# The one-hots of the repeated pairs are built on ScalarE, and most of a histogram is summed there: a graph network on one Trainium2 core

## The reference, cut to what matters

```python
x = layernorm(x + L0(x, src, dst, ...))          # one attention layer, softmax over the edges of a node
x = layernorm(x + L1(x, [src, dst], edge_attr_128, ...))   # edge_aggr = zeros.at[src].add(edge_attr_128), then an MLP
x = layernorm(x + L2(x, [src, dst], edge_attr_3, ...))     # three attention layers
x = layernorm(x + L3(x, src, dst, ...))
# L3, five times: agg = segment_sum(h[src], dst); h = relu(bn(relu(bn((h + agg) @ W1 + b1)) @ W2 + b2)) ...
```

## Time and profile before

| what | value |
|---|---|
| time, median of 3 runs | 9828.47 us (9817.87 to 9830.84) |
| the profiled execution | 9827.57 us |
| its span, first to last instruction | 9826.3 us |
| busy in it: PE / DVE / ACT / POOL | 6388.6 / 4378.2 / 3263.5 / 4526.1 us |
| `positions()` | about 175 to 484.8 us |
| `sort_rows()` | 484.8 to 1596.5 us |

### The profile page before, as it was taken

The page is one execution under the profiler, slowest core; times in us unless marked ns, Lnnn a source line. Parts: engine busy times, 40 slices in busy tenths (PEclk is TensorE's granted clock), DMA queues, the critical chain, the costliest instruction groups (busy, mean ns, idle before and its releaser), DMA issues. The chain is left out here.

```text
span 9826.3 us, 148779 instructions
## 1 busy us (share of the span) xinstructions
PE 6388.6 (65%) x38246; PEld 4633.5 (47%) x38247; DVE 4378.2 (45%) x11659; ACT 3263.5 (33%) x5847; POOL 4526.1 (46%) x4475
## 2 busy tenths in 40 slices
PE   1720003747768865766657665766659898989896
PEld 1710003722258844666656665666634444444443
DVE  3880003579977775555545554555540202020203
ACT  1000000049967744444444444444420202020202
POOL 2887777567720005777577774777710000000001
PEclk8555556878889987888888997888879898989898
DMA  4423336747754412333233332333336464646463
GB/s 112 110 83 106 105 104 165 205 135 209 209 170 122 128 49 66 85 84 84 67 88 85 84 84 70 84 84 84 85 92 202 124 202 127 200 127 199 128 199 112
DMA packets 1108444, 1192.58 MB, mean 121 GB/s; under 512 B 118455, under 2 KB 993350, under 8 KB 1107768
## 3 DMA queue, kind: packets, MB, share of 16 engines
q1 hardware_dynamic: 711988, 630.75, 21.9%
q0 software_dynamic: 150784, 336.22, 14.6%
q10 hardware_dynamic: 245444, 222.71, 8.1%
HBM read 974.87 MB, written 216.86 MB: 121 GB/s over the span
## 5 line engine op out<-in xcount | busy, mean ns | idle before, releaser
L1190 POOL DMA_INDIRECT ring<-gat_rows,src_idx x2496 | 2415.1, 968 | 1002.4 <-issue 999.7
L1311 PE MATMUL ps<-ring,xT_b 128*128 x8192 | 1289.5, 306 | 975.0 <-ACT xT_b L1397 971.0
L1311 PEld LDWEIGHTS ps<-ring,xT_b 128*128 128x128 f32 x8192 | 1115.2, 211 | 1107.1 <-issue 1103.7
L1389 ACT ACTIVATE xT_a<-xT_a,state 128x514 f32<-128x514 f32 x1024 | 740.0, 723 | 1865.9 <-SPq L1162 1270.1
L1301 PE MATMUL ps<-ident,s_col 128*128 128x128 f32 x8192 | 1228.5, 299 | 190.1 <-DVE s_col L1326 116.8
L1301 PEld LDWEIGHTS ps<-ident,s_col 128*128 128x128 f32 x8192 | 1142.8, 215 | 211.9 <-DVE s_col L1326 115.9
L1820 POOL TENSOR_TENSOR features<-xT_a,features 128x640 bf16<-128x640 f32 x50 | 82.6, 1656 | 2431.6 <-ACT features L1817 2431.2
L1617 PE MATMUL ps<-xT_b,features 128*128 128x504 f16 (+1 forms) x5655 | 1198.3, 367 | 0.0
L1359 DVE CUSTOM_DVE_ANT_0 xT_a<-ps,mask,xT_a 128x512 f32<-128x512 f32 x1024 | 765.8, 748 | 713.4 <-PE ps L1301 494.5
L684 POOL DMA_INDIRECT by_src<-ring,state x832 | 848.6, 1020 | 254.8 <-issue 253.1
L1461 PE MATMUL ps<-ring,xT_b 128*128 x2048 | 276.9, 304 | 982.1 <-DVE xT_b L1470 885.2
(11 more groups left out here) (376 smaller groups left out, 8012.3 us busy)
## 6 DMA issues: line engine op xcount, KB each, us to landing
dl_all<-dloc_rows ACTq DMA_DIRECT2D x1052, 128.0 KB, 3.1
xT_b<-adjacency SPq DMA_DIRECT2D x145, 882.0 KB, 4.7
xT_b<-adjacency SPq DMA_DIRECT2D x145, 756.0 KB, 4.6
adj_tile<-adjacency SPq DMA_DIRECT2D x102, 882.0 KB
adjacency<-xT_b ACTq DMA_DIRECT2D x319, 252.0 KB
adj_tile<-adjacency SPq DMA_DIRECT2D x100, 756.0 KB
ring<-by_src SPq DMA_DIRECT2D x52, 1040.0 KB
ring<-gathered SPq DMA_DIRECT2D x208, 260.0 KB
```

Source lines behind the costliest of these rows:

```text
L1190: pool.indirect_dma_start(ring[:, o:o + RC], None, table[:, :], bass.IndirectOffsetOnAxis(src_idx[:, t * W + u:t * W + u + 1], 0)).then_in ...
L1311: m = pe.matmul(bank(BO + v % 2, R), pw[v % 4][:, w * P:(w + 1) * P], ring[:, w * RC:][:, bass.ds(look(SLOT, u - 7), R)], start=w == 0, st ...
L1389: act.activation(um[u % 4], sm[u % 8], ACT.Identity, bias=S[:, ER:][:, bass.ds(look(BC, u), 1)]).then_inc(q["act_a"], 1)
```

## The change

In the first pass of `positions()`, of every three chunks DVE still compares and sums the first. For the other two it only compares, and ACT sums the hits by a Copy with an accumulator output. `extra_counts()` keeps DVE's preparation but for three conversions and a subtraction that go and two scalings that come (`at` becomes -`at`, `block` becomes 1 - `block`), drops the comparisons of line 630, and returns a function `make(v)` that builds tile v on ACT: Abs of (index + `at`) over 128 columns, Abs of (index + `block`) over 50, then Relu of (1 - x) over both, 178 columns of bf16, into one of eight buffers. `sort_rows()` calls it from group `LATE` = 12 on, 9 or 10 tiles behind each group's two copies, so that the 832 tiles are spread over 92 groups. PE multiplies tile by tile, and DVE's 52 copies out of PSUM stay.

```diff
--- before.py
+++ after.py
@@ -78,6 +78,7 @@
 assert QT * P == QC and NQ * QC == EH
 DUMP = NB * P
 RG = 4
+LATE = 12
 NT = 5
 WD = 504
 NWIN = -(-(NB * P) // WD)
@@ -540,11 +541,24 @@
                 load(n)
             for c in range(NQ):
                 dve.wait_ge(q[f"ld{c % 2}"], 32 * (c // 2 + 1))
-                if c >= 2:
-                    dve.wait_ge(q["eq"], c - 1)
-                dve.tensor_scalar(hit[c % 2], blk[c % 2], binid, 0.0, ALU.is_equal, ALU.add,
-                                  accum_out=hist[:, c:c + 1]).then_inc(q["eq"], 1)
+                if c % 3 == 0:
+                    if c >= 2:
+                        dve.wait_ge(q["eq"], c - 1)
+                    if c >= 3:
+                        dve.wait_ge(q["act_a"], c // 3 * 2 - 1)
+                    dve.tensor_scalar(hit[c % 2], blk[c % 2], binid, 0.0, ALU.is_equal, ALU.add,
+                                      accum_out=hist[:, c:c + 1]).then_inc(q["eq"], 1)
+                else:
+                    if c >= 2:
+                        dve.wait_ge(q["eq"], c - 1)
+                    if c >= 3:
+                        dve.wait_ge(q["act_a"], (c - 2) // 3 * 2 + (c - 2) % 3)
+                    dve.tensor_scalar(hit[c % 2], blk[c % 2], binid, None, ALU.is_equal).then_inc(q["eq"], 1)
+                    act.wait_ge(q["eq"], c + 1)
+                    act.activation(hit[c % 2], hit[c % 2], ACT.Copy, accum_out=hist[:, c:c + 1]
+                                   ).then_inc(q["act_a"], 1)
             dve.wait_ge(q["eq"], NQ)
+            dve.wait_ge(q["act_a"], NQ - -(-NQ // 3))
             s(dve, lambda: dve.tensor_reduce(total, hist, AX.X, ALU.add))
             s(pe, lambda: pe.matmul(PS[:, 1024:1025], before, total, start=True, stop=True))
             s(dve, lambda: dve.tensor_copy(first, PS[:, 1024:1025]))
@@ -602,14 +616,11 @@
 
             at, block = XTa[:, 3072:3072 + ET], XTa[:, 3072 + ET:3072 + 2 * ET]
             whole = XTa[:, 3072 + 2 * ET:3072 + 3 * ET].bitcast(I32)
...
+            room = 3072 + 2 * ET
+            size = P + NBP
+            one = [XTa[:, room + i * size // 2:room + (i + 1) * size // 2].bitcast(BF16) for i in range(8)]
+            off = [XTa[:, room + 4 * size + i * size:room + 4 * size + (i + 1) * size] for i in range(2)]
+            whole = XTa[:, 3072 + 2 * ET:3072 + 3 * ET].bitcast(I32)
...
-            s(dve, lambda: dve.tensor_copy(whole, at))
-            s(dve, lambda: dve.tensor_copy(at_b, whole))
-            s(dve, lambda: dve.tensor_scalar(block_b, block, 1.0, None, ALU.subtract))
-            s(dve, lambda: dve.tensor_copy(iota_b, iota_row[:, :]))
-            s.wait(dve)
-
-            def equal(out, n, ids):
-                return dve.tensor_tensor(out, iota_b[:, 0:n].rearrange("p (a n) -> p a n", a=1).to_broadcast([P, 8, n]),
-                                         ids.rearrange("p (t a) -> p t a", a=1).to_broadcast([P, 8, n]), ALU.is_equal)
-
-            def evict(r):
-                dve.wait_ge(q["product"], 2 * r + 2)
+            s(dve, lambda: dve.tensor_scalar(block, block, -1.0, 1.0, ALU.mult, ALU.add))
+            s(dve, lambda: dve.tensor_scalar(at, at, -1.0, None, ALU.mult))
+
+            def make(v):
+                if v == 0:
+                    s.wait(act)
+                if v >= 8:
+                    act.wait_ge(q["product"], v - 7)
+                act.activation(off[v % 2][:, 0:P], iota_row[:, :], ACT.Abs, bias=at[:, v:v + 1])
+                act.activation(off[v % 2][:, P:size], iota_row[:, 0:NBP], ACT.Abs, bias=block[:, v:v + 1]
+                               ).then_inc(q["act_a"], 1)
+                act.wait_ge(q["act_a"], v + 1)
+                act.activation(one[v % 8], off[v % 2], ACT.Relu, bias=1.0, scale=-1.0).then_inc(q["eq"], 1)
+
+            for r in range(NV):
+                dve.wait_ge(q["product"], (r + 1) * RUN)
                 dve.tensor_copy(extra[:, r * NBP:(r + 1) * NBP], PS[:, r % 4 * 512:r % 4 * 512 + NBP]
                                 ).then_inc(q["evac"], 1)
-
-            for g in range(2 * NV):
-                if g >= 3:
-                    dve.wait_ge(q["product"], g - 2)
-                equal(node[g % 3], P, at_b[:, g * 8:(g + 1) * 8])
-                equal(home[g % 3], NBP, block_b[:, g * 8:(g + 1) * 8]).then_inc(q["eq"], 1)
-                if g >= 4 and g % 2 == 0:
-                    evict(g // 2 - 2)
-            for r in (NV - 2, NV - 1):
-                evict(r)
-            s.wait(pe)
-            for g in range(2 * NV):
-                r = g // 2
-                if g % 2 == 0 and r >= 4:
+            for v in range(ET):
+                r = v // RUN
+                if v % RUN == 0 and r >= 4:
                     pe.wait_ge(q["evac"], r - 3)
-                pe.wait_ge(q["eq"], g + 1)
-                for u in range(8):
-                    m = pe.matmul(PS[:, r % 4 * 512:r % 4 * 512 + NBP], node[g % 3][:, u, :], home[g % 3][:, u, :],
-                                  start=g % 2 == 0 and u == 0, stop=g % 2 == 1 and u == 7)
-                m.then_inc(q["product"], 1)
+                pe.wait_ge(q["eq"], v + 1)
+                pe.matmul(PS[:, r % 4 * 512:r % 4 * 512 + NBP], one[v % 8][:, 0:P], one[v % 8][:, P:size],
+                          start=v % RUN == 0, stop=v % RUN == RUN - 1).then_inc(q["product"], 1)
+            return make
 
         def sort_rows():
 
@@ -669,7 +672,7 @@
                 if g == RG:
                     edge_scores(s)
                     source_steps(s)
-                    extra_counts(s)
+                    make = extra_counts(s)
                 src = rows_of[g * L1U * P:(g + 1) * L1U * P, :] if g < n - 1 else tail_rows
                 for eng in (sp, act):
                     if g >= RG:
@@ -677,6 +680,9 @@
                 sp.dma_start(buf(b)[:, :, 0:D], tiled(src)).then_inc(q[f"ld{b}"], 16)
                 for o, t in ((D, src_cols), (D + 1, dst_cols)):
                     act.activation(buf(b)[:, :, o], t[:, g * L1U:(g + 1) * L1U], ACT.Copy).then_inc(q["stage"], 1)
+                if g >= LATE:
+                    for v in range((g - LATE) * ET // (n - LATE), (g - LATE + 1) * ET // (n - LATE)):
+                        make(v)
                 pool.wait_ge(q[f"ld{b}"], 16 * (g // RG + 1))
                 pool.wait_ge(q["stage"], 2 * (g + 1))
                 settled(pool)
```

## The result

The changed kernel takes 9791.37 us (median of 5 runs, 9779.2 to 9792.79) against 9828.47 of the kernel before (5 runs, 9817.87 to 9830.85): ratio 0.9959, 95% interval 0.9946 to 0.9973. It is faster by 37 us, 0.4%; forecast were 9784 us. Lines behind the changed functions now have a number higher by 6; the scatter of line 684 is line 690.

The account below looks back on a forecast made before the run. POOL's successive instructions bound the scatter; DVE and PE end the numbering, POOL close behind. From 9827.57 us, -43.5 and -1.3 give 9782.8, or 9784 against the median, 0.45% less; range 9773 to 9801.

Parts of the forecast that it names:

- Line 630 and POOL: Scatter in `sort_rows()`: without line 630 on DVE, 116 scatters take 959 instead of 1334 ns, saving 43.5 us.
- The 10.3 us that the copies out of PSUM might have cost: Scatter: line 635's 52 copies of 199 ns, if each held POOL for its whole length; nothing was taken for them.
- ACT's tile: Scatter: two Abs and a Relu take ACT 925 ns a tile, 8.8 us in POOL's 10.1 a group, costing nothing.
- ACT the bound: Rival in the scatter: tiles above 1.117 us make ACT late; at 1.19 us, 60 us more, 9844 us. Chance 0.08.
- The table loads: Rival on ACT: Abs and Relu evict each other's tables, two loads of 1.283 us a tile, 11900 us. Chance 0.02.
- The numbering: `positions()`: -3.85 us from the earlier end plus 2.5 for comparisons, so -1.3 us (-3.85 to +8.9).
- The release behind POOL's last store: End of the numbering: POOL's last store, issued by 478.63, plus 2.33 us landing and barrier, gives 480.96 instead of 484.81.
- the size that had been taken for the comparisons: Numbering: 17 new DVE comparisons hold POOL by chance for 3.8 us together; 2.5 us were taken.
- The first pass: First pass of `positions()`: 2.97 us a chunk instead of 3.54, near 88 us instead of 103.
- the 14.7 us: Numbering: DVE's gain over 26 chunks, of which at most 3.85 count; rival that it shows in full, 9771 us, chance 0.03.
- a full lock: Rival in the numbering: POOL's gathers wait out each of 17 new comparisons, 12.7 us, giving 9794 us. Chance 0.08.
- What one of them saves or costs is carried to the end: Whole kernel: stages are parted by barriers, so the touched stages' differences, -43.5 and -1.3 us, reach the end.

Follow-up runs that it names:

- LATE = 40: The changed kernel with lower bounds on registers, ACT's tiles starting at group 40 instead of 12 (13 a group): 9942.73 us, one run.
- bounds only: The kernel before with a lower bound of 1 on registers that semaphore waits compare with: 9836.7 us, ratio 1.0004 to the kernel before.
- no counts, bounds: The changed kernel with register bounds, repeated-pair counts left out (no tiles, products or copies; `extra` set to 0): 9805.53 us, ratio 0.9959 to the kernel before.
- histogram only, bounds: The kernel before with register bounds and only the histogram's change, one-hots staying on DVE: 9836.67 us, ratio 1.0001.
- counts only, bounds: The kernel before with register bounds and only the one-hots' change, the histogram staying wholly on DVE: 9810.85 us, ratio 0.9979.
- change, bounds, pause: The changed kernel with register bounds and twelve 640-column index fills on POOL behind the last scatter: 9857.52 us, ratio 1.0015 to the kernel before.
- change, bounds: The changed kernel with a lower bound of 1 on registers that semaphore waits compare with: 9848.5 us, ratio 1.0015 to the kernel before.
- change, bounds, FIRST = 24: The changed kernel with register bounds, 24 instead of 32 tiles gathered in the numbering, the rest in the source sums: 9851.6 us, ratio 1.0004.
- the three disturbed ones of this kind: The changed kernel with register bounds and an added PE product per source-sums step (512 columns twice, 256 once): 11494.72, 11765.54 and 11479.6 us.

## Why the prediction was right, and where it was not

**Line 630 and POOL: right, within 3 us.** Forecast were 43.5 us; the start of the next stage moved by 43.3, the scatter's length by 44.1, and by 40.7 (1101.9 to 1061.2) and 43.2 (1103.2 to 1060.0) in two other pairs with and without line 630. The first 38 scatters stayed at 1139 ns (1155 before). The 10.3 us that the copies out of PSUM might have cost do not occur: the scatters take 957 ns with them about, and the scatter lasts 1059.7 us without any.

**ACT's tile: right.** 925 ns forecast, 902 between tiles measured: 386 + 321 + 351 against 387 + 336 + 350. The rival "ACT the bound" needs 1117; LATE = 40 made it come true and gave it its price. The table loads did not come.

**The numbering: two terms mis-sized, little lost.** Forecast were -1.3 us, measured +0.6 at its end, -0.2 in its own length, and -3.9 in the pair with bounds. The sign is thus not settled. The release behind POOL's last store was mis-sized: 3.5 us from its end to the next stage, where 2.33 were taken over from the end of the scatter. POOL's last store is issued by 481.86 instead of 478.63; of these 3.2 us 0.7 come from a later start of the numbering, and 2.5 are left, the size that had been taken for the comparisons. The first pass was mis-sized too: chunks start (271.0 - 188.4) / 25 = 3.30 us apart, not 2.97. With DVE's 1.31 us on the mean that leaves 5.3 us for a load in the 6.6 us of a buffer, where 4.64 were worked out from the earlier trace rows. That is 8 of the 14.7 us; as POOL set the end, it cost nothing. The 12.7 us of a full lock, which the prediction worked out as its upper end, did not occur: POOL's gathers beside the new comparisons are at 979 and 988 ns in the first pass, where the earlier trace rows had 950, and 61 x some 33 ns is 2 us.

**"What one of them saves or costs is carried to the end": the step that failed.** The sum carried the difference at the end of the scatter unchanged through 8.2 ms. That would have given 9785. The stages behind gave back 7 us net, more than all errors ahead of them. Nothing in the prediction limits this to 7, so that the time came out close is in part luck: with the bounds on registers the same change gave back all 44 and more, with a span of 9850.1 against 9830.7.

What is shown of this is where it is lost. All ten undisturbed traces in order of their source sums (us; "pauses" are PE's 31 waits between passes, "root waits" the waits of ACT's square root for DVE in the GIN layers, which are counted to the end of the kernel):

| kernel | source sums | PE busy | clock | pauses | adjacency | GIN layers | root waits |
|---|---|---|---|---|---|---|---|
| before | 386.2 | 276.9 | 0.87 | 96.9 | 721.9 | 2589.7 | 37.4 |
| bounds only | 390.4 | 282.2 | 0.86 | 95.8 | 718.8 | 2588.3 | 37.5 |
| after | 391.4 | 283.3 | 0.85 | 95.6 | 730.5 | 2588.5 | 37.4 |
| no counts, bounds | 392.6 | 286.1 | 0.85 | 94.0 | 721.6 | 2590.8 | 37.5 |
| histogram only, bounds | 393.8 | 287.2 | 0.84 | 94.2 | 721.7 | 2589.1 | 37.4 |
| counts only, bounds | 403.8 | 293.7 | 0.83 | 97.6 | 720.3 | 2591.5 | 37.5 |
| change, bounds, pause | 424.4 | 306.2 | 0.79 | 105.6 | 731.1 | 2603.2 | 52.3 |
| change, bounds | 425.3 | 308.4 | 0.79 | 104.3 | 731.6 | 2602.7 | 52.3 |
| change, bounds, FIRST = 24 | 428.1 | 312.2 | 0.78 | 103.3 | 731.6 | 2602.5 | 52.3 |
| change, bounds, LATE = 40 | 429.2 | 313.0 | 0.77 | 103.7 | 728.6 | 2604.4 | 52.3 |

The losses are not scattered from build to build. The four kernels that have both halves of the change and the bounds lose 21 to 43 us in the source sums and 11 to 16 in the GIN layers against all others, on two chips; the three disturbed ones of this kind have 2607.5 to 2608.1 us of GIN layers and 52.3 of root waits too, against 2593.1 and 37.4 of the kernel before beside two of them. In the GIN layers the loss is DVE's loop of statistics. In the source sums PE's pauses between passes are 3.33 to 3.41 us on the mean in these four and 3.03 to 3.15 in the others. That makes up 6 to 12 us, and PE's longer time at 1.2 GHz behind the pauses goes with the rest. Whether the longer pauses cause the lower clock is argued from this agreement; no run changes the pauses alone, and the runs that were to hold the clock up were disturbed.

What is not shown is why DVE's loops take longer in just these builds, as no edit touches their instructions, but for the bounds in the source sums. It is not the length of the scatter, not the start by 6 us and not POOL's share of gathers, all of which were changed without effect, and neither half of the change, nor both without the bounds, nor the bounds alone bring it about. Every one of these edits also puts DVE's loops at another place among its instructions; whether that matters, no run tests. The adjacency has a difference of its own, which the clock (0.85 to 0.86) doesn't explain: 728 to 732 us in every undisturbed kernel that has both halves of the change, with bounds or without, and 719 to 722 in all others. That stays open too.

## What to carry to other kernels

Where the engine that bounds a stage has its instructions lengthened beside those of another engine, the number of instructions times the difference is what moving that other work gains in the stage, and the receiving engine costs nothing up to a threshold that can be worked out from its slack per group. Speeding up a pass whose end is set by another engine pays only up to that engine. A saving of 0.4% can be lost in stages that the edit doesn't touch: here the same change came out at 0.9959 of the kernel before without the bounds and at 1.0015 with them. Compare stage by stage, judge the edit by its own stage before the total, and see in more than one build whether a loss far behind the edit comes back.

## What had not been expected of the hardware

The same 2048 products took 276.9 to 313.0 us of PE, the granted clock 0.87 to 0.77, with no change to their stage. A loop of one engine took 0.82 us a pass in some builds and 0.6 in others, with the same instructions. VectorE's one-input comparisons of 2048 columns (789 ns on the mean) hardly touch POOL's gathers (979 to 988 ns, 950 before), where line 630 with two inputs stretched the scatters from 959 to 1334. Reading ACT's accumulator takes 186 ns, DVE's 82. And in a disturbed run the wait of an engine for its own instruction before can go from 0.03 us to 2.4 us on the mean (131 times, 317 us), which a chain of many short waits pays each time.
